# A graph layer's edge loop: steps of 128 edges with eight additions a batch, and a rebuilt prologue

## The reference

```python
xn = _layernorm(x)
# graph attention
h = (xn @ W).reshape(n, 8, 32)
a1, a2 = sum(h * attn_l, -1), sum(h * attn_r, -1)
e = leaky_relu(a1[src] + a2[dst], 0.2)
ex = exp(e - segment_max(e, dst)[dst])
alpha = ex / segment_sum(ex, dst)[dst]
gnn = segment_sum(h[src] * alpha, dst) + bias
# mixing branch: q, k, v from xn @ W_qkv; q, k centred, squared, normalised
kv = einsum('bnc,bnd->bcd', k2, v);  t2 = einsum('bnc,bcd->bnd', q2, kv) / sqrt(N)
mix = (v + t2) @ W_out + b_out
x = x + gnn + mix
# two experts of eight for all tokens, gelu, weighted sum, layer norm
x = x + ffn(_layernorm(x))
```

## Time and profile before

| | |
|---|---|
| median of three runs | 2740.4 us |
| the profiled execution, its span | 2743.08 us, 2741.3 us |
| TensorE busy, VectorE, GpSimd, ScalarE | 76%, 64%, 61%, 32% |
| first gather of the edge loop, last | 124.5 us, 2271.1 us |
| granted TensorE clock, mean over the span | 0.844 |

### The profile page before, as it was taken

The page is one execution under the profiler, slowest core; times in us unless marked ns, Lnnn a source line. Parts: engine busy times, 40 slices in busy tenths (PEclk is TensorE's granted clock), DMA queues, the critical chain, the costliest instruction groups (busy, mean ns, idle before and its releaser), DMA issues.

```text
span 2741.3 us, 37518 instructions
## 1 busy us (share of the span) xinstructions
PE 2075.5 (76%) x8314; PEld 1415.2 (52%) x8315; DVE 1748.8 (64%) x3633; ACT 876.4 (32%) x1856; POOL 1672.4 (61%) x1764
## 2 busy tenths in 40 slices
PE   3777777777777777777777778788788773799997
PEld 2545545454554444455445455555555541477776
DVE  7566666666666666666666667777777667333334
ACT  1533333333333333333333332222222221433332
POOL 4177777777777777777777777777777771000000
PEclk9877888888788888887887878888878866899999
DMA  6655555555555555555555555555555551100000
GB/s 217 241 151 144 152 149 143 144 151 147 145 149 149 143 144 152 149 143 147 149 147 144 152 146 156 161 161 162 162 154 160 143 133 25 31 18 17 17 17 25
DMA packets 182669, 359.19 MB, mean 131 GB/s; under 512 B 39635, under 2 KB 92715, under 8 KB 182636
## 3 DMA queue, kind: packets, MB, share of 16 engines
q0 software_dynamic: 82848, 233.35, 32.0%
q1 hardware_dynamic: 98116, 123.87, 14.9%
q10 hardware_dynamic: 1672, 1.59, 0.2%
HBM read 325.91 MB, written 32.75 MB: 131 GB/s over the span
## 4 chain that ended last, share of the span: by engine, by line
PE 37%; issue 16%; DVE 16%; DMA 12%; ACT 11%; POOL 5%; DVEq 1%; SPq 0%; POOLq 0%; ACTq 0%
DMA work<-h_tab,idx 12%; PE bank L892 10%; PE bank L1005 6%; POOL work L579 5%; ACT work L676 5%; PE bank L995 4%; PE bank L901 4%; DVE zs L1270 4%; PE bank L910 3%; DVE acc L1300 2%; DVE zb L1272 2%; DVE zb L1273 2%; DVE zb L1271 2%; PE bank L899 1%; PE bank L944 1%
## 5 line engine op out<-in xcount | busy, mean ns | idle before, releaser
L579 POOL DMA_INDIRECT work<-h_tab,idx x1712 | 1626.0, 950 | 525.2 <-issue 444.0
L892 PE MATMUL bank<-work 128*128 128x264 f32 x3424 | 1074.0, 464 | 311.3 <-DVE acc L1300 304.7
L892 PEld LDWEIGHTS bank<-work 128*128 128x128 f32 x3424 | 729.0, 227 | 566.1 <-DVE acc L1300 408.2
L1292 DVE TENSOR_TENSOR work<-work,bank 128x1024 f32<-128x1024 f32 x428 | 520.4, 1216 | 168.7 <-issue 154.6
L1300 DVE TENSOR_TENSOR acc<-bank,acc 128x264 f32 x854 | 366.1, 429 | 285.4 <-PE bank L892 277.4
L684 ACT ACTIVATE bank<-zb 128x64 f32<-128x64 f32 x214 | 48.7, 228 | 1457.1 <-DVE zb L1275 1453.2
L1185 DVE TENSOR_TENSOR work<-bank,cols 128x1024 f32<-128x1024 f32 x215 | 261.1, 1215 | 0.0
L678 ACT ACTIVATE work<-work,ones 128x1024 bf16<-128x1024 bf16 x215 | 246.8, 1148 | 7.0
L676 ACT ACTIVATE work<-work,pcol 128x1024 bf16<-128x1024 bf16 x215 | 243.5, 1132 | 6.4 <-DMA work<-dst_d 6.4
L606 POOL COPY work<-acc 128x768 f32 (+2 forms) x17 | 13.6, 805 | 368.7 <-PE bank L957 295.8
L1270 DVE TENSOR_REDUCE zs<-bank 128x128 f32<-128x384 f32 x214 | 118.2, 552 | 165.7 <-DMA work<-h_tab,idx 165.2
(11 more groups left out here) (241 smaller groups left out, 1903.6 us busy)
## 6 DMA issues: line engine op xcount, KB each, us to landing
work<-dst_d SPq DMA_DIRECT2D x216, 256.0 KB, 3.8
work<-h_tab,idx POOLq DMA_INDIRECT x1712
xx_d<-acc SPq DMA_DIRECT2D x49, 256.0 KB, 2.1
xnt_c<-xx_d SPq DMA_DIRECT2D x66, 128.0 KB, 3.6
h_tab<-acc SPq DMA_DIRECT2D x49, 132.0 KB, 1.9
xn_c<-xx_d SPq DMA_DIRECT2D x49, 128.0 KB, 2.3
q2t_d<-q2t_c SPq DMA_DIRECT2D x49, 128.0 KB, 1.9
X<-x SPq DMA_DIRECT2D x6, 1024.0 KB, 11.9
```

The lines of the kernel that those rows point to most:

```text
L579: nc.gpsimd.indirect_dma_start(out=ring[q][:, j, :], out_offset=None, in_=h_tab, in_offset=bass.IndirectOffsetOnAxis(ap=idx[:, q, j:j + 1] ...
L892: ins = mm(bank[3 + s % 2][:, 0:TW], hot[q][:, s * G + g, :], ring[q][:, s * G + g, :], start=(g == 0), stop=(g == G - 1))
L1292: v.tensor_tensor(m, m, ex, ALU.mult).then_inc(msg_ready, 1)
```

## The change

A unit is 128 edges instead of 256 (`G = 1`), so a step has one matmul and one add, and a batch eight steps. 1612 units and 48 changes of tile make 1660 steps and 208 batches, where it was 806, 854 and 214. Sums rotate over three banks (3, 4, 0), three adds (`LAG`) go over into the next batch, and the adds stand at other places of VectorE's list. A sum s waits for the add s - 3. The one-hots of the batch stand behind add(0).

The prologue: x is loaded first, in two half chunks; normalising goes in seven groups of up to eight tiles (`ln_var`, `ln_root`); the loop over tiles is unrolled; the step table is counted from `below` (units whose last edge lies before a tile) and `past` (steps at or behind a tile's first), in three pieces among the tiles 1, 4 and 7; `t_acc` and `t_a2c` lie in one tensor; the conversion is at tile 43 and the turns behind it; GpSimd centres the weights ahead of its 28 fetches (14 before); ScalarE zeroes the accumulator's end, which was GpSimd's memset; the first gathers don't wait for the `xx_d` stores any more. The two attention columns are kept by one copy, and their order in `a2c` is exchanged.

```diff
-G = 2
+G = 1
-SB = 4
-LAG = 2
+SB = 8
+LAG = 3
+HS = SB // 2
+MB = [3, 4, 0]
 ...
+            sp.dma_start(X[:, 0:HX, :], xv[:, 0:HX, :]).then_inc(x_loaded[0], 16)
+            sp.dma_start(X[:, HX:XC, :], xv[:, HX:XC, :]).then_inc(x_loaded[7], 16)
             sp.wait_ge(lastd_clear, 1)
 ...
-            nc.gpsimd.memset(acc[:, A_COLS:], 0.0).then_inc(acc_zero, 1)
 ...
-            for stored in (h_stored, xx_stored):
-                all_stored(pool, stored)
+            all_stored(pool, h_stored)
 ...
+            act.wait_ge(lastd_clear, 1)
+            nc.scalar.copy(acc[:, A_COLS:], small[:, 31:32].to_broadcast([P, NT * TW - A_COLS])).then_inc(acc_zero, 1)
 ...
                 for s in range(SB):
-                    if s % 2 == 0:
-                        pe.wait_ge(msg_ready, b * 2 + s // 2 + 1)
+                    if s % HS == 0:
+                        pe.wait_ge(msg_ready, b * 2 + s // HS + 1)
                     if s == 0:
                         pe.wait_ge(den_ready, b + 1)
-                    wait(pe, added, b * SB + s - 1)
+                    wait(pe, added, b * SB + s + 1 - len(MB))
                     for g in range(G):
-                        ins = mm(bank[3 + s % 2][:, 0:TW], hot[q][:, s * G + g, :], ring[q][:, s * G + g, :],
+                        ins = mm(bank[MB[(q * SB + s) % len(MB)]][:, 0:TW], hot[q][:, s * G + g, :], ring[q][:, s * G + g, :],
                                  start=(g == 0), stop=(g == G - 1))
 ...
+            def lows():
+                v.tensor_copy(kio, iotai).then_inc(dve_own, 1)
 ...
+                own(v.tensor_copy(lastf, lastd))
+                v.tensor_tensor(below, lastf.unsqueeze(2).to_broadcast([P, UCH, NT]),
+                                tlow.unsqueeze(1).to_broadcast([P, UCH, NT]), ALU.is_lt).then_inc(below_ready, 1)
+            def pasts():
+                dve.wait_ge(tiles_counted, 1)
+                own(v.tensor_tensor(first[0:NT], bank[7][0:NT, 480:481], ucol[0:NT, 0:1], ALU.add))
+                v.tensor_scalar(past[0:NT, :], kio[0:NT, :], first[0:NT], None, ALU.is_ge).then_inc(past_ready, 1)
+            def units():
+                dve.wait_ge(steps_counted, 1)
 ...
+                for r, k in enumerate(ROWS):
+                    v.tensor_scalar(t_acc[:, r * ROW:(r + 1) * ROW], bank[k][0:1, 0:ROW], -1.0, float(TW), ALU.add, ALU.mult)
 ...
                 dve.wait_ge(ex_ready, b + 1)
                 scale(0)
                 if not begin:
+                    add(-3)
                     add(-2)
                 scale(1)
                 if not begin:
                     add(-1)
+                add(0)
                 if not last:
                     one_hots(b + 2, (q + 2) % R3)
 ...
-                add(0)
+                add(1)
+                add(2)
                 if not last:
                     exponents(b + 1, (q + 1) % R3, i + 1 if q < 2 else i + 2)
-                add(1)
+                add(3)
+                add(4)
```

More of the change, by code:

```diff
@@ L386, in build @@
         NWG, NW = 3, 9
+        LN = [(g * A1, g * A1 + A1) for g in range(NT // A1)] + [(NT - 1, NT)]
+        LN_AT = [g * A1 + 5 for g in range(NT // A1)]
         TT = 3
-        TA = A1 * Q_MID
+        T_CONVERT = 43
+        T_TURN = T_CONVERT + 3
         def phases(eng, batch):
@@ L407, in phases, with first_pass @@
             batch(IT, 0, "", False)
[L409 to L420, removed]
+        def first_pass(tile):
+            for t in range(NT):
+                tile(t, t % A1, t // A1)
         def table_chunks(t):
-            n = t - (TA - TT) if isinstance(t, int) else -1
+            n = t - T_TURN
             return range(KCH * n // TT, KCH * (n + 1) // TT) if 0 <= n < TT else ()
@@ L810, in tile @@
             def tile(t, p, n):
[L811 removed]
+                if t + 1 < NT:
                     xn_in(t + 1, (p + 1) % A1)
@@ L817, in tile @@
                 ins.then_inc(h_made, 1)
+                if t == 3:
+                    pe.wait_ge(below_ready, 1)
+                    for c in range(UCH):
+                        ins = mm(bank[7][0:NT, 480:481], below[:, c, :], ones[:, 0:1], start=(c == 0), stop=(c == UCH - 1))
+                    ins.then_inc(tiles_counted, 1)
+                if t == 6:
+                    pe.wait_ge(past_ready, 1)
+                    for c in range(KCH):
+                        mm(bank[7][:, ROW + c:ROW + c + 1], past[0:NT, c * P:(c + 1) * P], ones[0:NT, 0:1], start=True, stop=True)
+                    for r, k in enumerate(ROWS):
+                        ins = mm(bank[k][0:33, 0:ROW], ones[0:NT, 0:33], past[0:NT, r * ROW:(r + 1) * ROW], start=True, stop=True)
+                    ins.then_inc(steps_counted, 1)
                 for c in table_chunks(t):
@@ L827, in _ @@
             xn_in(0, 0)
-            for _ in first_pass(pe, tile):
-                xn_in(TA, 0)
+            first_pass(tile)
             pe.wait_ge(w_loaded, 16 * NW)
@@ new lines, in _ @@
+            dve.wait_ge(x_loaded[0], 16)
+            for t in range(A1 // 2):
+                measure(t)
+            dve.wait_ge(x_loaded[7], 16)
+            for t in range(A1 // 2, A1):
+                measure(t)
+            dve.wait_ge(x_measured, A1)
+            ln_var(own, *ln_of(0))
+            dve.wait_ge(w_loaded, 16 * NW)
+            v.tensor_reduce(small[:, 0:4].rearrange("p (k a) -> p k a", a=2),
+                            wqkv[:, :, 0:2 * C].rearrange("p k (a n) -> p k a n", a=2), AX.X, ALU.add).then_inc(w_summed, 1)
@@ L1162, in convert @@
                 v.tensor_copy(b_dst.rearrange("p c e -> p (c e)"), f_dst.rearrange("p c e -> p (c e)")).then_inc(dst_kept, 1)
-            early_tiles = True
-            for _ in first_pass(dve, tile):
-                early_tiles = False
-                v.bn_stats(stat[:, NT - 1, :], X[:, NT - 1, :]).then_inc(x_measured, 1)
-                dve.wait_ge(x_measured, NT)
-                ln_stats(own, 1, stat[:, TA:NT, :], [sc[:, n, TA:NT] for n in range(4)], mean[:, TA:NT], rstd[:, TA:NT])
+            first_pass(tile)
             for t in range(NT - 3, NT):
@@ L1384, in _ @@
                     if e == (c - 1) * XP:
-                        ln_stats(own, 2 + n, stat[:, a:e, :], [sc[:, k, a:e] for k in range(4)], mean[:, a:e], rstd[:, a:e])
+                        ln_stats(own, len(LN) + n, stat[:, a:e, :], [sc[:, k, a:e] for k in range(4)], mean[:, a:e], rstd[:, a:e])
                         own(v.scalar_tensor_tensor(out=sc[:, 3, a:e], in0=mean[:, a:e], scalar=-1.0, in1=rstd[:, a:e],
```

244 lines of the change are left out of this document (121 added, 123 removed).

## The result

The changed kernel takes 3130.2 us (median of 4 runs, 3124.6 to 3135.4) where the kernel before takes 2740.8 on the same chip: ratio 1.142, 95% interval 1.140 to 1.145. The forecast was 2832 us, slower, with a range from 2695 to 2900. The sign was right; the loss is 390 us where 92 were forecast.

The account below looks back on a forecast made before the run. GpSimd's gathers, one every 1.2546 us, were taken to pace the loop. 2743.1 - 60.2 + 142 + 41 - 27 + 1 = 2840, so 2837 as median, rounded down to 2832 us; range 2695 to 2900.

Parts of the forecast that it names:

- Gathers, -60.2: Edge loop: 48 gathers fewer at GpSimd's 1.2546 us each save 60.2 us, if GpSimd keeps the pace.
- The second add of a pair, 0.52: VectorE's batch: an add directly behind the one it waits for costs 0.52 us, within 0.34 to 0.57.
- The rival in which this wait is free: Pairs of adds: waiting inside a pair costs nothing, adds cost +1.36 us a batch; 2737 us, no change; 6%.
- The register load, taken at 0.70: VectorE's batch: one load of eight values idles 0.70 us as with four; 1.4 if delay goes by value.
- The waits for sums, forecast at 3.8 a turn: VectorE's q/k turn: waits for TensorE's sums fall from 5.3 to 3.8 us, between 1.3 and 5.3.
- 22.9 + 3 x 2.1 + 3.8 = 33.0: q/k turn of three batches: VectorE's work, dearer adds and waits make 33.0 us against GpSimd's 30.11; +142 us.
- which is in the shortened waits already: Sums: three banks let TensorE run two sums ahead of the adds, counted within the shortened waits, no separate term.
- A mixing batch, 10.88: Mixing stage: 8.38 + 2.1 us of work plus 0.4 of waits make 10.88, 0.84 over 10.04; +41 us.
- The clock falls, or loads cost by the value: Rival for the edge loop: no wait is given back, turn 34.8, mixing batch 11.7; +314, up to 2968 us; 17%.
- The prologue, -27: Ahead of the edge loop: first tile near 18, last copy near 91; net 27 us earlier, between 12 and 36.
- Expected signs: Trace after: gathers every 1.31 to 1.37 us waiting on sums, long add(0) wait two batches in three, first gather near 97.
- GpSimd keeps the pace: Rival for the edge loop: the turn stays under GpSimd's 30.11 us, so the kernel takes 2654 us; 7%.

Follow-up runs that it names:

- e11: Changed kernel with register load in two halves, additions spread between the exponents' steps, one-hots ahead of add(-1) and add(0): 2674.6 us, ratio 0.977 to the kernel before.
- e12: Kernel before with a register load of eight values instead of four in each batch, the last four unused: 2738.0 us, ratio 1.000.
- e3: Kernel before with register loads of eight values instead of four, on a chip where it takes 3217 us: 3223.5 us, ratio 1.002.
- e13: Changed kernel with only the register load split in two halves, on a slower chip: 3275.6 us, ratio 1.018 to the kernel before.
- e8: Changed kernel's rebuilt prologue and three banks with the batches of before (four additions of 256 edges): 2718.2 us, ratio 0.992 to the kernel before.

## Why the prediction was right in sign and wrong in size

The profiled run took 3135.4 us where the sum had 2840. Its terms, from the traces:

| term | forecast | measured |
|---|---|---|
| loop, 2146.6 us before | -60 +142 +41 = +123 | 2525.0: +378 |
| first gather, 124.5 before | -27 | -2 |
| behind the last gather, 470.2 before | +1 | 485.6: +15 |
| sum | +97 | +392 |

The 15 us at the end weren't followed up; in e11 that stretch takes 474.0.

- **Gathers, -60.2.** Right only if GpSimd paces; e11 collects it: its loop is 2082.7 us, 63.9 under the earlier trace rows.
- **The second add of a pair, 0.52.** It is 0.62 to 0.63 (1029.83 to 1030.45), above both bounds. The rival in which this wait is free is refuted: 410 waits of 0.20 us. The sentence of the Trainium skill behind it ("VectorE: DVE Perf Modes", "The DRAIN you can't avoid") is on a semaphore set behind each of eight copies; it doesn't hold for this wait, and the measurement decides. (The prediction's "some 80 us" for this end doesn't fit its own rival, which lies 2837 - 2737 = 100 us lower.)
- **The register load, taken at 0.70.** It is 1.63. This is the largest miss among the terms: 4.8 us a turn for 2.1. With it and the pairs' 1.8 a turn the list fills 25.0 (busy) + 4.8 + 1.8 + 3.6 (sums) = 35.2 of the 35.9 us.
- **The waits for sums, forecast at 3.8 a turn.** They are 3.6, but not as forecast: one long wait a turn, not two, and about half of the 139 waits are the 0.20 inside a pair. The size is right by luck.
- **The step that failed** is the turn made as a sum over VectorE's list: "22.9 + 3 x 2.1 + 3.8 = 33.0". First, its load term was mis-sized. At 1.63 the load adds 2.8 us a turn and 0.9 a mixing batch, the pairs at 0.62 add 1.2 and 0.4: 49 x 4.0 + 49 x 1.3 = 260 us, as much as the 255 by which the loop exceeded its forecast. Second, such a sum doesn't say what a term is worth, and TensorE's side was settled by "which is in the shortened waits already". An engine waits for what it isn't doing, so its list fills any turn, and that the mended sum comes out right proves little: the load doubled costs nothing in the kernel before (e12, e3), the load hidden in the changed one comes back as waits (e13). The changed kernel's own chain goes through one register load of three, 93 us in the q/k stage and 4.1% of the span, 128 us, in all. By that chain it is the most that the load can explain of the 392; the other loads lie where the chain runs through other engines. What is left is the ring through both engines: sums, three banks, additions behind the one-hots and the exponents, and the side work and picks behind the last sum. One bank less costs 586 us with the same list of VectorE, and the same instructions in another order, with the load hidden, save 456.
- **What stays open.** That the loss lies in VectorE's order, pairs and load together is shown (e11). The size of each where before takes 2740 us is not: alone they were run only on the slower chips (order 57 us, spreading 20 to 23, load 0 to 5, of 85). There hiding the load won nothing (e13); where before takes 2740 us its worth lies, by the chain, somewhere between nothing and 128 us.
- **A mixing batch, 10.88.** 12.9. The wait for sums is 62.7 us in 46.6 batches, 1.3 where 0.4 was kept, and the load's idle is 80.0 us, 1.7 a batch where 0.7 was kept.
- **The rival "The clock falls, or loads cost by the value", 2968.** It names the cause of the largest miss, but its sum, 22.9 + 6.6 + 5.3, has no term for the loads. At 1.4 a load, as the prediction has it elsewhere, it would be 2.1 us more a turn and 0.7 a mixing batch: 49 x 2.8 = 137, so 3105, near the measured time. Some of that nearness is luck, as its waits of 5.3 were 3.6.
- **The clock.** It fell, 0.75 and 0.79 for 0.82 and 0.86. In e11 the same matmuls over the same three banks have 0.84, so neither their number nor their banks bring it down; TensorE's pauses go with it. How much of the loss the lower clock adds isn't separated: in the changed kernel a record of a sum takes 515 ns in the mean, before 464. The rule cited from "TensorE: Matmul & The Clock Gate" of the Trainium skill, that a turning through banks with small pauses makes the clock swing, fits: 0.75 with the pauses, 0.84 without.
- **The prologue, -27.** The first tile came at 18.76, as forecast (18). Between it and the last tile the stalls on the counts and the root, 19.3 us, weren't in the 73. With the table of 14 fetches (e8) the first gather comes at 104.4, with 28 fetches and twice the conversions at 122.5, and at 115.5 in e11, which has the same prologue. Of those 7 us 4.9 are there when TensorE goes on with the tiles behind the counts, at 55.64 us and in e11 at 50.73: from 18 to 40 us the granted clock was 0.84 in the changed kernel and 1.00 in e11, from 40 to 60 us 0.57 and 0.66. Why it differs in the same code isn't settled.
- **Expected signs.** Idle before gathers on TensorE's sums and no waits for gathers: seen. The long wait at add(0) was there in one batch of three, not in two. The second add came 0.62 behind the first, not 0.5 to 0.57. The spacing of 1.31 to 1.37 was 1.52, the first gather near 97 came at 122.5.
- **GpSimd keeps the pace**, 2654 at 7%, was false for this order of VectorE's list and nearly true for the next one: 2675.

## What to carry to other kernels

When two engines hand banks to each other, don't price a change by adding up one engine's list: its waits fill any turn, and the sum says nothing of what a term is worth. Follow the ring: which result must be taken before the producer can go on, and what stands ahead of the taking. If more and smaller handovers are made, spread the taking among the consumer's other work, one behind each short step, and put work that others need ahead of a taking that waits. A wait of before that nobody felt (TensorE's for the additions, hidden under GpSimd's pace) is where the ring will bind. And don't carry the cost of an instruction over to another size: the load of four values had 0.70 us of idle time, that of eight 1.63.

## What the runs showed of the hardware

- VectorE's register load leaves 0.77 us of idle time in the mean with four values (107.2 us in 139 waits, 140 to 1610 us of the kernel before; mostly 0.70) and 1.63 to 1.65 with eight (changed kernel, e12): 0.9 us for four more. A semaphore wait on VectorE's own last instruction adds 0.20 us, 0.28 from start to start (0.62 against 0.34).
- Of the five chips of the experiments four run the kernel before 17 to 18% slower, with waits that the trace ascribes to no engine of this core. The changed kernel loses 5% on the one of them where it ran, so the same edit is worth 14% on one chip and 2% on another.
